# A bidirectional Mamba, attention and spectral block on one core: dt·x moves from VectorE to GpSimd, and one decay moves to another PSUM buffer

## The reference, cut to what matters

```python
def _mamba_dir(x, W_in, conv_w, conv_b, W_x, W_dt, b_dt, A_log, D, W_out):
    xz = x @ W_in;  xp, z = xz[..., :128], xz[..., 128:]
    xc = silu(xprev * conv_w[:, 0] + xp * conv_w[:, 1] + conv_b)
    dt_r, Bc, Cc = split(xc @ W_x)               # 8, 16 and 16 columns
    dt = softplus(dt_r @ W_dt + b_dt);  A = -exp(A_log)
    h = exp(dt_t[:, :, None] * A) * h + (dt_t * x_t)[:, :, None] * B_t[:, None, :]   # for each t
    y = einsum('bds,bs->bd', h, C_t)
    return ((y + D * xc) * silu(z)) @ W_out
```

## Time and profile before

| | us |
|---|---|
| median of 3 runs (959.43 to 964.2) | 961.29 |
| the profiled execution's own time | 963.2 |
| its span | 961.4 |
| busy in the span: TensorE matmuls | 832.3 |
| VectorE | 711.4 |
| ScalarE | 511.7 |
| GpSimd | 549.7 |

### The profile page before, as it was taken

How to read it: one execution, slowest core, us unless ns; L and a number is a source line. 1 busy time by engine, 2 the same in 40 slices (tenths; PEclk the granted TensorE clock), 3 DMA queues, 4 the chain that set the end, 5 groups by cost and what they waited for, 6 DMA issues and landing times. The chain is left out here.

```text
span 961.4 us, 10231 instructions
## 1 busy us (share of the span) xinstructions
PE 832.3 (87%) x3004; PEld 491.3 (51%) x3004; DVE 711.4 (74%) x767; ACT 511.7 (53%) x706; POOL 549.7 (57%) x373
## 2 busy tenths in 40 slices
PE   5578897979898898975679898949999999999996
PEld 1223333433333343422235455528888888888885
DVE  1999999999999999999953464526656655565664
ACT  4645656666566656643225356545554554555553
POOL 4678989999998999965646943411122121222210
PEclk9799999999999999997898899979999999999998
DMA  7869897889879897875329300001433333243441
GB/s 183 320 226 327 315 331 275 350 302 316 304 287 353 294 331 280 350 277 209 135 29 154 107 1 0 1 1 44 132 97 121 131 100 120 88 129 93 128 117 58
DMA packets 75349, 178.24 MB, mean 185 GB/s; under 512 B 24514, under 2 KB 25044, under 8 KB 75300
## 3 DMA queue, kind: packets, MB, share of 16 engines
q1 hardware_dynamic: 75316, 177.85, 56.5%
HBM read 175.57 MB, written 2.26 MB: 185 GB/s over the span
## 5 line engine op out<-in xcount | busy, mean ns | idle before, releaser
L455 POOL TENSOR_TENSOR prod<-hidden,c_wide 128x1024 f32<-128x1024 f32 x128 | 300.1, 2357 | 64.4 <-DVE hidden L888 61.6
L551 PE MATMUL ps_y<-prod,ident 128*128 128x512 f32 x512 | 242.0, 616 | 33.1 <-POOL prod L455 32.9
L888 DVE TENSOR_TENSOR_SCAN hidden<-decay,ps_d 128x1024 f32<-128x1024 f32 x92 | 209.9, 2282 | 8.3
L1856 PE MATMUL ps_conv<-hankel,u_high 128*128 128x512 f32 (+1 forms) x768 | 215.4, 361 | 0.0
L551 PEld LDWEIGHTS ps_y<-prod,ident 128*128 128x128 f32 x512 | 97.5, 196 | 173.0 <-issue 115.4
L1856 PEld LDWEIGHTS ps_conv<-hankel,u_high 128*128 128x128 f32 x768 | 138.7, 189 | 25.4 <-issue 0.3
L2016 DVE TENSOR_TENSOR stack<-ps_conv,stack 64x512 fp32r<-64x512 f32 x128 | 88.3, 690 | 68.7 <-ACT stack L1979 66.3
L1856 PE MATMUL ps_conv<-hankel,u_low 128*128 128x512 f32 (+1 forms) x384 | 138.1, 360 | 0.0
L1739 POOL CAST block_mix<-even 128x256 fp32r (+1 forms) x32 | 12.7, 398 | 218.7 <-PE ps_tail L1838 218.7
L2016 DVE TENSOR_TENSOR qk<-ps_conv,qk 64x512 fp32r<-64x512 f32 x128 | 88.3, 690 | 50.0 <-ACT qk L1979 47.2
L1979 ACT ACTIVATE stack<-ps_conv 64x512 fp32r<-64x512 f32 x128 | 76.0, 594 | 82.2 <-PE ps_conv L1856 80.3
(11 more groups left out here) (307 smaller groups left out, 1189.9 us busy)
## 6 DMA issues: line engine op xcount, KB each, us to landing
b_wide<-bc_rows SPq DMA_DIRECT2D x128, 512.0 KB, 5.5
c_wide<-bc_rows SPq DMA_DIRECT2D x128, 512.0 KB, 5.4
hankel<-filters SPq DMA_DIRECT2D x32, 1026.0 KB, 5.3
plus<-in_M_phi_plus SPq DMA_DIRECT2D x2, 1024.0 KB, 14.0
minus<-in_M_phi_minus SPq DMA_DIRECT2D x2, 1024.0 KB, 18.0
x_pair<-in_x SPq DMA_DIRECT2D x2, 768.0 KB, 8.2
bc_rows<-mixed_and_low SPq DMA_DIRECT2D x8, 128.0 KB, 5.6
out<-plus SPq DMA_DIRECT2D x4, 256.0 KB, 4.9
```

The lines of the kernel that those rows point to most:

```text
L455: nc.gpsimd.tensor_tensor(prod[k % PAIR][:, :], hidden[k % DEEP][:, :], c_wide[s % BC_DEEP][:, :], ALU.mult).then_inc(prod_ready, 1)
L551: mm = nc.tensor.matmul(out, ident[:, :], halves(prod[k % PAIR])[h], start=False, stop=(k % N == N - 1))
L888: nc.vector.tensor_tensor_scan(hidden[k % DEEP][:, order], left[:, order], right[:, order], 0.0, ALU.mult, ALU.add).then_inc(hidden_ready, 1)
L1856: mm = nc.tensor.matmul(out, pairs[q][wp][:, 2 * delta + source, :], rows, start=(delta == 0 and term == 0), stop=(delta == 2 * half + 1 a ...
```

## The change

GpSimd makes dt·x of the next unit in memory (`dtx` from `dt` and `xc`) after product 12 and after the drive of state 15. ScalarE copies `dtx` to `ps_x` at state 15, where it had copied the other way. VectorE no longer makes dt·x, and starts a unit when `ps_x` is filled. The decay of state 15 goes to `ps_w` instead of `ps_d`, directly after dt has been taken from there; so TensorE's next writes to `ps_w` also wait for scan 15. Unit 0 keeps its old way of making dt·x.

```diff
+PSUM_W_DECAYS = POOL_STATES[1:]
+DTX_AT = 12
...
+                def dt_x(u, i):
+                    pool.wait_ge(dt_ready, u + 1)
+                    pool.wait_ge(dtx_ready, u)
+                    pool.wait_ge(share_ready, SHARE * u)
+                    nc.gpsimd.tensor_tensor(dtx[:, :], dt[i][:, :], xc[i][:, :], ALU.mult).then_inc(dtx_kept, 1)
...
                             if s + SHARE_AHEAD - N in shared(last and i == 0) and not (last and i == 1):
                                 share(u + 1, s + SHARE_AHEAD - N)
+                            if s == DTX_AT and not (last and i == 1):
+                                dt_x(u + 1, 1 - i)
                             if not first:
                                 if i == 0 and s == 12:
                                     norm_rstd(nc, pool, g, a.minus_half, b - 1)
...
                 def gate_in(u, i, b):
                     pe.wait_ge(dtx_ready, u)
+                    at_least(pe, hidden_ready, N * (u - 1))
                     project(i, b, w_gate[i], z_ready)
...
-                def keep_dtx(u):
-                    act.wait_ge(dtx_ready, u + 1)
-                    at_least(act, share_ready, SHARE * u)
-                    nc.scalar.activation(dtx[:, :], ps_x[:, :], ACT.Copy).then_inc(dtx_kept, 1)
+                def spread_dtx(u):
+                    act.wait_ge(dtx_kept, u + 1)
+                    act.wait_ge(drive_ready, driven_before(u - 1, N - 2) + 1)
+                    nc.scalar.activation(ps_x[:, :], dtx[:, :], ACT.Copy).then_inc(dtx_ready, 1)
...
-                    nc.scalar.activation((ps_w if s in WIDE_SHARED else ps_d)[:, :], dt[i][:, :], ACT.Exp,
+                    nc.scalar.activation((ps_w if s in PSUM_W_DECAYS else ps_d)[:, :], dt[i][:, :], ACT.Exp,
...
                             if s == 13:
                                 take_dt(v, j)
+                                shared_decay_of(u, i, POOL_STATES[4], dt_ready, v + 1)
                             if s == N - 1:
-                                shared_decay_of(u, i, POOL_STATES[4], hidden_ready, u * N + POOL_STATES[4])
-                                keep_dtx(v)
+                                spread_dtx(v)
                                 decay_of(v, j, 1, last and i == 0)
...
-                def dt_x(u, i):
-                    dve.wait_ge(dt_ready, u + 1)
-                    dve.wait_ge(dtx_kept, u)
-                    dve.wait_ge(drive_ready, driven_before(u - 1, N - 2) + 1)
-                    nc.vector.tensor_tensor(ps_x[:, :], ps_w[:, :], xc[i][:, :], ALU.mult).then_inc(dtx_ready, 1)
...
                         if not (first and i == 0):
-                            dve.wait_ge(dtx_kept, u + 1)
+                            dve.wait_ge(dtx_ready, u + 1)
...
-                            if s == N - 2 and not final:
-                                dt_x(u + 1, 1 - i)
```

More of the change, by code:

```diff
@@ L607, in tokens @@
                     pe.wait_ge(dtx_ready, 2 * B)
+                    pe.wait_ge(hidden_ready, N * (2 * B - 1))
                     for t in range(TILES):
@@ L724, in take_dt, with keep_first_dtx @@
                     nc.scalar.activation(dt[i][:, :], ps_w[:, :], ACT.Copy).then_inc(dt_ready, 1)
-                def keep_dtx(u):
-                    act.wait_ge(dtx_ready, u + 1)
-                    at_least(act, share_ready, SHARE * u)
+                def keep_first_dtx():
+                    act.wait_ge(dtx_ready, 1)
                     nc.scalar.activation(dtx[:, :], ps_x[:, :], ACT.Copy).then_inc(dtx_kept, 1)
+                def spread_dtx(u):
+                    act.wait_ge(dtx_kept, u + 1)
+                    act.wait_ge(drive_ready, driven_before(u - 1, N - 2) + 1)
+                    nc.scalar.activation(ps_x[:, :], dtx[:, :], ACT.Copy).then_inc(dtx_ready, 1)
                 def decay_of(u, i, s, last=False):
@@ L828, in _ @@
                 act.wait_ge(drive_ready, 1)
-                keep_dtx(0)
+                keep_first_dtx()
                 act.wait_ge(consts, CONSTS)
@@ L882, in scan_step @@
                         dve.wait_ge(share_ready, shared_before(u, s, final) + 1)
-                        left, right = (ps_w if s in WIDE_SHARED else ps_d), drive[DRIVE_OF[s]]
+                        left, right = (ps_w if s in PSUM_W_DECAYS else ps_d), drive[DRIVE_OF[s]]
                     else:
```

## The result

The changed kernel takes 969.36 us (median of 8 runs, 967.38 to 973.82) against 960.62 for the kernel before in its 8 runs: 1.0093 times as long, interval 1.0071 to 1.0115, so 6.8 to 11.0 us slower. Forecast were 967.5 us and +6.2. The profiled execution has a span of 966.7 us. One execution of experiment e7, the one that was profiled, took 1647.1 us where its ten others took 964.7 to 969.7; it is left out of every comparison, and e7b is the same kernel again.

The account below looks back on a forecast made before the run. VectorE was taken to set the pace, GpSimd close behind, with 0.32 us of slack from product 15 to scan 2. Boundary losses less 1.27 us gave +6.2 us, so 967.5 us against the 961.29 median; range 960.5 to 974.

Parts of the forecast that it names:

- VectorE's 8.9 us are free, but no path leads there: VectorE loses dt·x, 1.27 us in each of 7 units; in six this becomes waiting at scan 2.
- Product 15 late, decay of state 2 behind the taking of z: Unit boundaries: product 15 comes 1.05 to 1.85 us later, slack is 0.32 us, so ScalarE's decay delays scan 2.
- the sum: Boundary losses of units 0 to 5 less 1.27 us kept in unit 6: +6.2 us.
- The terms of unit 0 and unit 5: Boundaries after these units: dt comes after the drive, putting product 15 past the slack by 1.43 and 1.52 us.
- ScalarE's copy: Memory to PSUM at state 15: 1.02 us, covered by scan 15, priced at 0.
- TensorE's new waits: Waits for scan 15 before `gate_in` and unit 7's tokens: behind the sum of product 15, priced at 0.
- the decay's move: Decay of state 15 in `ps_w`, moved to about 242.9: 1.12 us of otherwise idle ScalarE, priced at 0.
- GpSimd catches up inside the unit: Products 0 to 11 absorb the lateness; 5.7 us of idle time allow for 2.3, so delays do not accumulate.
- SyncE's queue at 0: Loads of B behind delayed loads of C: asked some 13 us ahead, landing in 5.5; 0, ends 0 and 1 us.
- a sign of being wrong in size: In the new profile: scan 2's wait being another than forecast, or a drive waiting for `b_wide`.
- The clock rival: TensorE at its lower level for product 15's sum and `gate_in`, half of six boundaries: 976.5 us; chance 0.12.
- the boundary term: Unit boundaries: the late product 15 makes scan 2 wait, +6.2 us, the whole forecast loss.

Follow-up runs that it names:

- e7: The kernel before with the decay of state 15 moved to `ps_w`, TensorE's waits for scan 15, and VectorE's dt·x reading dt from memory; 965.36 us.
- e7b: The same kernel as e7, run again for a profile; 965.48 us, 1.0073 of the kernel before.
- e3: The changed kernel with GpSimd's multiply of dt and x cut from 1024 columns to 8, all waits kept; 952.44 us.
- e1: The changed kernel with the decay of state 2 put ahead of the taking of z in ScalarE's queue; 956.51 us.
- e5: The kernel before with one more GpSimd multiply, result unused, where the change puts dt·x; VectorE's dt·x stays; 971.14 us.
- e6: e5 with the decay of state 2 ahead of the taking of z in ScalarE's queue; 962.25 us.
- e4: The changed kernel with TensorE computing each batch's output product twice, to fill its idle time; 970.33 us.
- e8: e1 with each load of C one state later in SyncE's queue and one more load of C at the end; 956.78 us.
- e9: The kernel before with only VectorE's dt·x reading dt from memory instead of `ps_w`; 968.2 us.

## Why the prediction was right, and where it was not

- **VectorE's 8.9 us are free, but no path leads there.** Right: e3 takes 7.8 us less than the kernel before (960.26, measured beside it), and e1 7.8 us less at the boundaries.
- **Product 15 late, decay of state 2 behind the taking of z.** Right in place and in order, shown by e1, e3, e5 and e6. The size: boundaries +4.7 us where the sum gave +6.2. From unit 0 on they are longer by 0.6, 0.6, 1.3, 0.7, 1.9, 0.7 and −1.1 us, where the sum has 1.4, 0.7, 1.5, 0.7, 1.5, 1.5 and −1.3. Scan 2 waits 2.03, 1.98, 2.56, 2.10, 2.56 and 2.16 us in units 1 to 6 where I had 2.7, 2.0, 2.8, 2.0, 2.8 and 2.8. The terms of unit 0 and unit 5 were too large (1.43 and 1.52 forecast, 0.56 and 0.74 measured): I had priced dt as late there because TensorE's clock was low in the profile I read, and where the low clock falls changes from profile to profile. e4 shows the opposite draw.
- **ScalarE's copy** starts at 249.26 and takes 1.03 us; only e1 and e8, where VectorE is no longer held up, show a drive waiting for it, by 0.4 and 0.3 us. **TensorE's new waits** and **the decay's move**: no cost shows, as priced (e7 against e9).
- **GpSimd catches up inside the unit; SyncE's queue at 0.** This step failed, 7.0 us in the profile of the changed kernel. I took a B as asked for some 13 us ahead, four states of average length. In the trace of the kernel before the mean over units 1 to 6 is 10.3 us, and for state 10 of an even unit it is 5.8 to 6.1, with 5.5 needed. A drive that waits for `b_wide` is what the prediction itself named as a sign of being wrong in size, and it came. The clock rival had the right cause, a low clock after idleness, at the wrong place: on the boundary pair of sum and `gate_in`, which took 1.98 and 1.88 us at all six boundaries, and not on the groups behind VectorE's new wait. (In e9 the sum of that pair was slow at two boundaries.)
- **The total.** 8.7 us against 6.2: the boundary term was 1.5 us too large, and the missing term is 7.0 in one profile. Between the two profiles the recurrence lost 11.2 us (463.4 against 452.2), but the spans differ by only 5.3, because the stretch after it was 4.5 us shorter and the first scan came 1.4 us earlier. The place and the mechanism of the first loss followed from the rows; that the total came within 2 us of the forecast is in part luck, an error upwards against a missing term.

## What to carry to other kernels

An engine with idle time on average may have none at the place where its product is the first link of a chain; ask of each moved instruction what stands behind it in its queue, and follow that to the engine that sets the pace. Where a late result reaches that engine only because an unrelated instruction is queued behind its consumer, reorder that queue first: here one swap was worth some 12 to 13 us (969.36 against 956.51). And look at each load's lead at its tightest state, not on average.

## What the runs showed of the hardware that I had not expected

- A VectorE multiply with both inputs in memory and a GpSimd multiply hold each other up: 3.89 us instead of 1.21, or 3.26 instead of 2.36 for GpSimd (e9, and the same in e7b). With one input in PSUM, as in the kernel before, neither shows. The Trainium skill's "SBUF — State Buffer", section "Who interferes with whom", states that a `tensor_tensor` with both inputs in SBUF contends with GpSimd's reads; the traces agree. In unit 2 dt·x outlasted not only the product that was running but the next one too, which is more than one instruction's hold.
- TensorE fell to half its clock after an idle time of 4.2 to 4.6 us in each of units 1 to 6 of the changed kernel (convolution's input 3.75 to 3.78 us). With the idle time filled in units 2, 4 and 6 (e4, 0.9 to 1.0 us left) it did not there (1.96 to 1.99 us), while units 1, 3 and 5 of the same profile, with 4.6 us left, still did. After 2.1 to 2.3 us of idle time at the same place (e1, e8) some units were slow and some not.
- A loss of TensorE's clock of about 2.8 us on two groups was passed on through three engines and two queues, and arrived at VectorE as 1.4 to 1.9 us of waiting for a load.
